# Loading each expert's weights in three transfers, spreading the low parts anew, and starting TensorE on constants earlier, in a fused convolution, attention and expert kernel

## The chip, the cores and the metric

The kernel runs on one core of a Trainium2 chip. The metric is the device time of one execution in microseconds (us); a smaller number is better. The kernel before took 234.52 us as the median of three runs (233.04 to 238.59).

## What is computed

The input x is a batch of 8 images with 192 channels and 16 x 16 pixels, in float32. Three stages follow one another:

```python
x = x + conv1x1(concat(gn(x), corr(gn(x))))   # gn over 32 groups; corr: 28 products of a normalised pixel with neighbours
t = tokens(x)                                 # 8 images x 256 tokens x 192
t = t + softmax(causal(q @ k.T / sqrt(192))) @ v   # q, k, v from the layer-normed t
g = ln(t) @ Wg.T + bg; e = argmax(g)          # one of 8 experts for each token, weight 1
t = t + (silu(ln(t) @ W1[e].T) * (ln(t) @ W2[e].T)) @ W3[e].T   # inner width 469
```

## The kernel before

Each engine has an instruction stream of its own, written out by hand, and the streams meet only at semaphores. SyncE (SP) issues the direct transfers, GpSimd (POOL) the indirect ones.

**Split products.** TensorE reads rounded numbers ("fp32r"). To keep the accuracy of float32, an operand is split into a high part (a rounded copy) and a low part (the original minus the high part), and TensorE sums several products of parts. The eight experts' weights, 1,324 KB each, arrive as float32 in one of two staging places (`stage[:, e % 2]`, 2,648 columns: 940 for channels 0 to 127 of W1 and W2, 940 for the remaining 64 channels in two copies, 768 for W3) and are written split into `wall[:, e]`. ScalarE writes the three high parts (`weights_hi`, lines 549, 551 and 554; semaphores `wall_hi`, `wall_hiq`, `wall_hi3`). GpSimd writes the low parts of the first and the third range (`weights_lo`, lines 434 and 437; `wall_lo` after both), and VectorE turns the second copy in the second range into low parts (`leftover`, line 837; `wall_q`). For experts 6 and 7 all low parts are made by VectorE later, in the expert stage, in six pieces each (`low_weights`, lines 821, 824, 829).

**Staging.** A place is free once the expert that lies in it has been split. SP waits in order for `wall_lo` and `wall_q` of expert e - 2 and then issues the whole of expert e (`weights_in`, line 300, loop of lines 336 to 339). Expert 0 is loaded earlier in four quarters, between the images' own transfers. ScalarE's `weights_hi` waits for the one semaphore of the place (line 547).

**Start.** SP issues the image transfers and the constants. POOL fills constants (lines 372 to 375, the tile `taps` last), and counts each on `filled`. TensorE waits for the fourth, then runs `keep_busy(3)` on `taps` (line 1336): products of constants into a bank that nobody reads, each seen as two instructions of 384 columns. Then come `group_sums(0)` (line 1141, the sums of the group norm of images 0 and 1, which VectorE's `group_factors` at line 728 waits for), `keep_busy(5)`, and `group_sums(1)` for images 2 to 4.

**Convolution stage.** Twelve steps, pipelined over the images: group norm and split (lines 515, 523, 738), neighbour products (1205 to 1209), norms, a round trip of the products through memory to shear them (`gram_to`, `taps_from`), convolution.

**Attention stage.** `step(t)` for t from 1 to 9 works on image t's projections and image t - 1's softmax. ScalarE's order in a step is: copy of the turned image (559), `weights_hi(1)` and `weights_hi(2)` of expert t - 1, the exponentials (585, 586), copies (564, 592), the norm of the next image (613), values (570, 573), `weights_hi(0)` of expert t. TensorE fills in with unread products (`fill`, line 1278). At t = 4, 6, 7, 8 and 9 VectorE also computes gates and positions of tokens, and POOL scatters the token rows by expert.

**Expert stage.** 23 slots of 128 tokens, at least one for each expert. In slot j (`ffn_step`) TensorE turns the previous slot's hidden rows (line 1429), multiplies by W1 and W2 (1146 to 1150, 2 x 5 products of 470 columns), turns the next slot's tokens (1446) and multiplies the previous slot's hidden values by W3 (1468, 1469). VectorE writes the low part HL of the hidden values (1084), the product gh (1089), the low part FL of the tokens (1092), the norm of the slot after next (1078, 1079) and the output rows (1105, 1107). VectorE's pieces of `low_weights` stand at the end of its part of slots 0 to 5, two in each: expert 6 in slots 0 to 2, expert 7 in slots 3 to 5. In slot 0 TensorE has `fill(8)` between the products and the turning.

## Time and profile before

| | |
|---|---|
| median of 3 runs | 234.52 us (233.04 to 238.59) |
| profiled execution, its own time | 233.54 us |
| its span, first to last instruction | 231.7 us |
| TensorE busy | 209.1 us, 90% |
| VectorE busy | 171.4 us, 74% |
| ScalarE busy | 113.9 us, 49% |
| GpSimd busy | 105.3 us, 45% |
| share of the chain that ended last | TensorE 59%, VectorE 16%, POOL 6%, DMA 6%, ScalarE 5% |

The profiled execution lies 1.0 us below the median of the three runs. The 1.84 us between its time and its span lie outside the instructions. A share of busy time is a mean over stages with different limits: the convolution stage ends near 60 us, the attention stage near 126 us, and the expert stage takes the rest. Part of TensorE's busy time is unread products.

### The profile page before, as it was taken

To read this page: it belongs to the slowest core of one execution; us is meant where nothing else is said; L and a number is where in the kernel's file an instruction comes from. 1 tells how busy PE (TensorE), PEld (TensorE's weight loads), DVE (VectorE), ACT (ScalarE), POOL (GpSimd) and SP (SyncE) were. 2 spreads that over 40 slices of the span, in tenths; PEclk is the share of its full clock that TensorE was granted. 3 is DMA by queue.
4 is the path that set the end of the run, shared out by engine and by line. 5 is a ranking of instruction groups with operands and counts; after the bars stand their busy time and mean duration, and the time that the engine had idled before them with its cause. 6 is when DMAs were issued, how large, how long until landed. Compare 5 with 4: busy or idle time off the path is not lost.

```text
span 231.7 us, 4547 instructions
## 1 busy us (share of the span) xinstructions
PE 209.1 (90%) x1331; PEld 182.4 (79%) x1331; DVE 171.4 (74%) x559; ACT 113.9 (49%) x244; POOL 105.3 (45%) x133
## 2 busy tenths in 40 slices
PE   6999799989899969998888799999999999999950
PEld 3686588968799958887665688898999999999940
DVE  3577897768399769699877789997767686868640
ACT  2276585175499697996640134343343333343410
POOL 4245756545439996896665103223131313131221
PEclk9999999999999999999999999999999999999995
DMA  6992247665730663647212332332001000000000
GB/s 218 366 350 87 83 126 187 170 219 165 252 135 0 237 234 117 221 188 259 81 52 63 80 86 70 93 83 78 21 14 37 17 34 20 34 17 22 33 20 0
DMA packets 16343, 26.46 MB, mean 114 GB/s; under 512 B 3795, under 2 KB 12673, under 8 KB 15424
## 3 DMA queue, kind: packets, MB, share of 16 engines
q1 hardware_dynamic: 14448, 22.65, 30.7%
q0 software_dynamic: 1872, 3.52, 4.4%
q8 instruction: 12, 0.20, 0.4%
q14 instruction: 11, 0.09, 0.2%
HBM read 19.76 MB, written 6.76 MB: 114 GB/s over the span
## 4 chain that ended last, share of the span: by engine, by line
PE 59%; DVE 16%; POOL 6%; issue 6%; DMA 6%; ACT 5%; POOLq 1%; DVEq 0%; ACTq 0%
PE bank L1468 8%; PE bank L1146 4%; PE bank L1333 4%; PE bank L1150 4%; PE bank L1149 4%; PE bank L1148 4%; PE bank L1147 4%; PE bank L1429 4%; PE bank L1469 3%; DMA stage<-in_w_all 2%; PE bank L1446 2%; PE bank L1192 2%; DMA taps_sb<-near_rows 2%; DMA out_rows<-yo,rows 1%; PE bank L1141 1%
## 5 line engine op out<-in xcount | busy, mean ns | idle before, releaser
L498 POOL DMA_INDIRECT out_rows<-yo,rows x23 | 23.2, 1011 | 76.9 <-DVE yo L1107 61.5
L1468 PE MATMUL bank<-wall,HH 128*128 (+1 forms) x88 | 28.1, 374 | 0.3 <-issue 0.3
L667 ACT ACTIVATE HH<-bank 128x512 fp32r<-128x512 f32 x23 | 13.8, 599 | 27.8 <-PE bank L1429 27.7
L1089 DVE TENSOR_TENSOR gh<-gh,bank 128x470 f32<-128x470 f32 x23 | 14.8, 645 | 14.5 <-PE bank L1150 14.4
L673 ACT ACTIVATE FH<-bank 128x256 fp32r<-128x256 f32 x23 | 8.9, 385 | 27.5 <-PE bank L1446 27.5
L1469 PE MATMUL bank<-wall,HL 128*128 (+1 forms) x88 | 22.1, 251 | 0.0
L1146 PE MATMUL bank<-wall,FH 128*128 (+1 forms) x46 | 19.3, 419 | 1.6 <-DVE FL L1092 1.6
L464 POOL DMA_INDIRECT token_rows<-rows,posi x16 | 16.9, 1055 | 7.3 <-issue 4.0
L670 ACT ACTIVATE gh<-bank 128x470 f32<-128x470 f32 x23 | 13.0, 565 | 13.1 <-PE bank L1150 13.1
L1278 PE MATMUL bank<-mH 128*128 128x512 f32 x73 | 19.3, 400 | 0.0
L1084 DVE TENSOR_TENSOR HL<-bank,HH 128x512 fp32r<-128x512 f32 x23 | 15.9, 691 | 3.6 <-ACT HH L667 3.4
L1150 PE MATMUL bank<-wall,FL 128*128 (+1 forms) x46 | 17.3, 376 | 0.0
L1149 PE MATMUL bank<-wall,FH 128*128 (+1 forms) x46 | 17.2, 375 | 0.0
L1148 PE MATMUL bank<-wall,FL 128*128 (+1 forms) x46 | 17.2, 375 | 0.0
L1147 PE MATMUL bank<-wall,FH 128*128 (+1 forms) x46 | 17.2, 374 | 0.0
L1468 PEld LDWEIGHTS bank<-wall,HH 128*128 128x128 f32 x88 | 16.5, 188 | 0.8 <-issue 0.8
L1469 PEld LDWEIGHTS bank<-wall,HL 128*128 128x128 f32 x88 | 16.8, 191 | 0.0
L434 POOL TENSOR_TENSOR wall<-stage,wall 128x940 fp32r<-128x940 f32 x6 | 13.6, 2261 | 3.0 <-ACT wall L549 1.8
L1278 PEld LDWEIGHTS bank<-mH 128*128 128x128 f32 x73 | 13.1, 188 | 2.1
L1429 PE MATMUL bank<-small_sb,gh 128*128 128x128 f32 x92 | 13.8, 272 | 0.0
L515 ACT ACTIVATE f32t<-xcm,gnb,grs 128x256 f32<-128x256 f32 x16 | 8.7, 594 | 9.6 <-POOL gnb L392 9.6
L437 POOL TENSOR_TENSOR wall<-stage,wall 128x768 fp32r<-128x768 f32 x6 | 12.8, 2136 | 0.0
(247 smaller groups left out, 647.4 us busy)
## 6 DMA issues: line engine op xcount, KB each, us to landing
stage<-in_w_all SPq DMA_DIRECT2D x7, 1324.0 KB, 5.7
rows<-token_rows SPq DMA_DIRECT2D x23, 98.0 KB, 2.0
near_rows<-gram SPq DMA_DIRECT2D x8, 243.0 KB, 3.2
xcm<-in_x_cm SPq DMA_DIRECT2D x2, 768.0 KB, 8.3
rows<-in_x_tm SPq DMA_DIRECT2D x1, 1536.0 KB, 14.0
stage<-in_w_all SPq DMA_DIRECT2D x4, 331.0 KB, 4.0
token_rows<-emptyt SPq DMA_DIRECT2D x3, 294.0 KB, 4.2
taps_sb<-near_rows SPq DMA_DIRECT2D x8, 103.0 KB, 2.1
```

Source lines behind the costliest of these rows:

```text
L464: pool.indirect_dma_start(out=xs, out_offset=bass.IndirectOffsetOnAxis(ap=posi[:, j:j + 1].bitcast(U32), axis=0), in_=rows[:, j], in_offse ...
L498: pool.indirect_dma_start(out=out, out_offset=bass.IndirectOffsetOnAxis(ap=rows[:, j, C + 2:C + 3].bitcast(U32), axis=0), in_=yo[:, par], ...
L1084: nc.vector.tensor_tensor(HL[:, 1 - par].rearrange("p k x -> p (k x)"), bank[5][:], HH[:, 1 - par].rearrange("p k x -> p (k x)").bitcast(F ...
L1146: nc.tensor.matmul(dst, xh_a, y_a, start=True, stop=False)
L1147: nc.tensor.matmul(dst, xh_a, yl_a, start=False, stop=False)
L1148: nc.tensor.matmul(dst, xl_a, y_a, start=False, stop=False)
L1149: nc.tensor.matmul(dst, xh_b, y_q, start=False, stop=False)
L1150: return nc.tensor.matmul(dst, xl_b, y_q, start=False, stop=not more)
L1278: nc.tensor.matmul(bank[6][:], mH[:, 0:P], mH[:], start=True, stop=True)
L1429: mm = nc.tensor.transpose(bank[5][:, P * k:P * (k + 1)], gh[:, 1 - par, P * k:P * (k + 1)], ident)
L1468: nc.tensor.matmul(dst[:, 0:2 * C], HH[:, 1 - par, k], w(0, P, c0, c0 + 2 * C), start=(k == 0), stop=False)
L1469: mm = nc.tensor.matmul(dst[:, 0:C], HL[:, 1 - par, k], w(0, P, c0, c0 + C), start=False, stop=(k == FT - 1))
```

## The change

Each expert from 1 on is issued in three transfers, the three ranges of the staging place, each with a semaphore of its own; from expert 2 on, each is issued as soon as that range of the expert before has been read. POOL gets a further semaphore, `wall_lo_a`, after its first subtraction. Low pieces 4 and 5 of expert 6 move to the steps of slots -1 and 0 (so slot 0 has three pieces), expert 7's first four pieces move to slots 2 and 3, and its last two stand singly in slots 4 and 5; the waits at the head of `low_weights` are now issued in each call. POOL fills `taps` first, TensorE starts after it, with `keep_busy(6)` in place of 3, and `fill(8)` in slot 0 becomes `fill(5)`. Expert 0 keeps its quarters, under a semaphore of its own.

```diff
+        PARTS = (slice(0, W12), slice(W12, 2 * W12), slice(2 * W12, STAGE))
...
-            def weights_in(e):
-                sp.dma_start(stage[:, e % 2], w_all[e]).then_inc(stage_in[e % 2], 16)
+            def weights_in(e, part):
+                c = PARTS[part]
+                sp.dma_start(stage[:, e % 2, c], w_all[e][:, c]).then_inc(stage_in[e % 2][part], 16)
...
-            weights_in(1)
+            for part in range(3):
+                weights_in(1, part)
 
             for e in range(2, EXPERTS):
+                sp.wait_ge(wall_lo_a, e - 1)
+                weights_in(e, 0)
+                sp.wait_ge(wall_q, e - 1)
+                weights_in(e, 1)
                 sp.wait_ge(wall_lo, e - 1)
-                sp.wait_ge(wall_q, e - 1)
-                weights_in(e)
+                weights_in(e, 2)
...
         def _(pool):
+            nc.gpsimd.memset(taps[:].rearrange("p b h c -> p (b h c)"), 1.0).then_inc(filled, 1)
             nc.gpsimd.memset(half_c[:], -0.5).then_inc(filled, 1)
             nc.gpsimd.memset(emptyt[:], 0.0).then_inc(filled, 1)
             nc.gpsimd.memset(gram[:].rearrange("p b h c -> p (b h c)"), 0.0).then_inc(filled, 1)
-            nc.gpsimd.memset(taps[:].rearrange("p b h c -> p (b h c)"), 1.0).then_inc(filled, 1)
-            pool.wait_ge(filled, 2)
+            pool.wait_ge(filled, 3)
...
-                nc.gpsimd.tensor_tensor(w[:, W12:2 * W12], raw[:, 0:W12], w[:, 0:W12].bitcast(F32), ALU.subtract)
+                nc.gpsimd.tensor_tensor(w[:, W12:2 * W12], raw[:, 0:W12], w[:, 0:W12].bitcast(F32), ALU.subtract).then_inc(wall_lo_a, 1)
...
-                sc.wait_ge(stage_in[e % 2], 16 * (e // 2 + (1 if e % 2 else FIRST_PARTS)))
+                if e == 0:
+                    sc.wait_ge(first_in, 16 * FIRST_PARTS)
+                else:
+                    sc.wait_ge(stage_in[e % 2][part], 16 * ((e + 1) // 2))
...
+                ve.wait_ge(wall_hi, e + 1)
+                ve.wait_ge(wall_hiq, e + 1)
+                ve.wait_ge(wall_hi3, e + 1)
+                ve.wait_ge(wall_lo, e)
                 for n in pieces:
-                    if n == 0:
-                        ve.wait_ge(wall_hi, e + 1)
...
                 if j == -1:
                     ffn_step(j, 1, False, False, True)
                     table_slots()
+                    low_weights(EXPERTS - 2, (4,))
                 elif j == 0:
                     ffn_step(j, 0, False, True, False)
                     norm_slot(1, 1, 1)
+                    low_weights(EXPERTS - 2, (5,))
                     ffn_step(j, 0, False, False, True, 2)
...
-                if 0 <= j < 3:
+                if 0 <= j < 2:
                     low_weights(EXPERTS - 2, (2 * j, 2 * j + 1))
-                elif 3 <= j < 6:
-                    low_weights(EXPERTS - 1, (2 * j - 6, 2 * j - 5))
+                elif 2 <= j < 6:
+                    low_weights(EXPERTS - 1, ((0, 1), (2, 3), (4,), (5,))[j - 2])
...
-            pe.wait_ge(filled, 4)
-            keep_busy(3, taps[:].rearrange("p b h c -> p (b h c)"))
+            pe.wait_ge(filled, 1)
+            keep_busy(6, taps[:].rearrange("p b h c -> p (b h c)"))
...
                 if j == 0:
-                    fill(8)
+                    fill(5)
```

## Rows read from the trace of the kernel before

**Rows 1.** The page: busy time, share of the span and instructions of each engine.
```profile
PE 209.1 (90%) x1331; PEld 182.4 (79%) x1331; DVE 171.4 (74%) x559; ACT 113.9 (49%) x244; POOL 105.3 (45%) x133
```
**Rows 2.** The waits: engine, line, who was waited for, total us, times, longest us.
```profile
ACT wall L549 <- DMA stage<-in_w_all: 2.2, 2, 1.8
```
**Rows 3.** Timeline of ScalarE, end of attention step 3: start us, duration us.
```profile
81.21 0.99 ACT L549 ACTIVATE wall<-stage 128x940 fp32r<-128x940 f32 x1 [1.80 <-DMA stage<-in_w_all]
```
**Rows 4.** Timelines of POOL and VectorE: expert 1's low parts.
```profile
70.47 2.21 POOL L434 TENSOR_TENSOR wall<-stage,wall 128x940 fp32r<-128x940 f32 x1
72.63 2.76 POOL L437 TENSOR_TENSOR wall<-stage,wall 128x768 fp32r<-128x768 f32 x1
...
71.29 2.38 DVE L837 TENSOR_TENSOR wall<-stage,wall 64x940 fp32r<-64x940 f32 x1
```
**Rows 5.** The chain that ended last, at expert 3's transfer: start us, us.
```profile
75.42 5.71 DMA stage<-in_w_all
```
**Rows 6.** The issues of transfers: count, KB each, median us from issue to landing.
```profile
stage<-in_w_all SPq DMA_DIRECT2D x7, 1324.0 KB, 5.7
...
stage<-in_w_all SPq DMA_DIRECT2D x4, 331.0 KB, 4.0
```
**Rows 7.** Timeline of TensorE in attention step 4.
```profile
83.70 0.39 PE L1234 MATMUL bank<-XH,mH 128*128 128x256 f32 x1 [1.52 <-DVE XH L800]
```
**Rows 8.** The chain that ended last, turning of gh in slots 2 to 4.
```profile
142.22 0.44 PE bank L1429 x4
...
146.56 0.44 PE bank L1429 x4
...
150.52 0.44 PE bank L1429 x4
```
**Rows 9.** Timeline of all engines in slot 2, around the last two pieces of expert 6.
```profile
143.16 1.21 DVE L829 TENSOR_TENSOR wall<-stage,wall 64x470 fp32r<-64x470 f32 x2
...
144.40 0.69 DVE L1084 TENSOR_TENSOR HL<-bank,HH 128x512 fp32r<-128x512 f32 x1
...
145.16 0.19 PEld L1468 LDWEIGHTS bank<-wall,HH 128*128 128x128 f32 x1 [0.36 <-issue]
```
**Rows 10.** Timeline of all engines in slot 0.
```profile
131.38 2.02 PE L1278 MATMUL bank<-mH 128*128 128x512 f32 x8
131.58 0.65 DVE L1089 TENSOR_TENSOR gh<-gh,bank 128x470 f32<-128x470 f32 x1 [0.83 <-PE bank L1150]
...
132.43 0.31 DVE L1079 TENSOR_SCALAR xf<-rows 128x64 f32<-128x64 f32 x1
...
133.23 0.38 PE L1446 MATMUL bank<-small_sb,xf 128*128 128x128 f32 x2
...
134.07 0.42 DVE L1092 TENSOR_TENSOR FL<-bank,FH 128x256 fp32r<-128x256 f32 x1 [1.33 <-ACT FH L673]
```
**Rows 11.** Timeline of the first 15 us: constants' products, group sums, and what waits.
```profile
1.79 0.45 POOL L375 MEMSET taps_sb<- 128x416 f32 x1
...
2.29 4.21 PE L1333 MATMUL bank<-taps_sb 128*128 128x384 f32 x6 [2.29 <-POOL taps_sb L375]
...
6.29 1.72 PE L1141 MATMUL bank<-mq,small_sb 128*128 128x8 f32 x8
...
11.06 1.16 PEld L1333 LDWEIGHTS bank<-small_sb 128*128 128x128 f32 x4 [0.17 <-issue]
...
12.68 0.96 PE L1141 MATMUL bank<-mq,small_sb 128*128 128x12 f32 x8
...
13.67 0.25 DVE L728 TENSOR_REDUCE mv<-bank 128x6 f32<-128x12 f32 x2 [0.74 <-PE bank L1141]
14.24 0.68 DVE L738 TENSOR_TENSOR f<-f32t,f 128x512 fp32r<-128x512 f32 x1
```
**Rows 12.** Granted clock by stretch: us, busy by engine, clock, DMA share, GB/s.
```profile
2.30:3.30 1.00, 1.00 (x2) 0.70 (x3) 0.00 (x0) 0.00 (x0) 0.69 (x5) 1.00 0.90 340
...
120.00:220.00 100.00, 96.85 (x575) 86.90 (x576) 77.55 (x213) 35.05 (x68) 26.09 (x28) 1.00 0.16 47
```

More of the change, by code:

```diff
@@ L242, in build @@
         cm_in = [sem(f"cm_in{g}") for g in range(len(GANGS))]
-        stage_in = [sem("stage_in0"), sem("stage_in1")]
+        first_in = sem("first_in")
+        stage_in = [[sem(f"stage_in{par}{part}") for part in range(3)] for par in range(2)]
+        wall_lo_a = sem("wall_lo_a")
+        PARTS = (slice(0, W12), slice(W12, 2 * W12), slice(2 * W12, STAGE))
         empty_out = sem("empty_out")
@@ L329, in _ @@
                     c = slice(n * (b - 2), n * (b - 1))
-                    sp.dma_start(stage[:, 0, c], w_all[0][:, c]).then_inc(stage_in[0], 16)
+                    sp.dma_start(stage[:, 0, c], w_all[0][:, c]).then_inc(first_in, 16)
                 if 4 <= b < 4 + HEAD_PARTS:
@@ L760, in take_gram @@
                 ve.wait_ge(rn_ready, b + 1)
-                ve.wait_ge(filled, 3)
+                ve.wait_ge(filled, 4)
                 if b >= 2:
@@ L812, in low_weights @@
                 raw3 = raw[:, 2 * W12:STAGE].rearrange("p (k c) -> p k c", c=C)
+                ve.wait_ge(wall_hi, e + 1)
+                ve.wait_ge(wall_hiq, e + 1)
+                ve.wait_ge(wall_hi3, e + 1)
+                ve.wait_ge(wall_lo, e)
                 for n in pieces:
-                    if n == 0:
-                        ve.wait_ge(wall_hi, e + 1)
-                        ve.wait_ge(wall_hiq, e + 1)
-                        ve.wait_ge(wall_hi3, e + 1)
-                        ve.wait_ge(wall_lo, e)
                     if n < 2:
@@ L1333, in keep_busy @@
                     nc.tensor.matmul(bank[6][:, 0:3 * P], some[:, 0:P], some[:, 0:3 * P], start=True, stop=True)
-            pe.wait_ge(filled, 4)
-            keep_busy(3, taps[:].rearrange("p b h c -> p (b h c)"))
+            pe.wait_ge(filled, 1)
+            keep_busy(6, taps[:].rearrange("p b h c -> p (b h c)"))
             pe.wait_ge(group_in, 16)
```

## The prediction

> **What bounds the kernel now.** I read the shares of the engines first. TensorE is busy for 90% of the span [rows 1], but many of its products are unread, so the share alone does not say that it is the bound. I therefore went to the waits and the timelines of the three places that the change touches. For the attention stage the list of waits shows ScalarE stopped at line 549 by a transfer of weights, 2.2 us in two waits, the longer one 1.8 us [rows 2]. The timeline places it: ScalarE stands still for 1.80 us until expert 3 has landed, and only then reads it [rows 3]. Behind that instruction in ScalarE's queue stands the copy of the turned image of step 4, for which VectorE and then TensorE wait: TensorE idles for 1.52 us at its projection [rows 7]. The expert stage is bound by TensorE, with a slot of about 3.9 us; the turning of gh comes 4.34 us after the one before in slot 3 and 3.96 us in slot 4 [rows 8], and the reason lies in slot 2. In the first 15 us the chain runs through the group sums and through constants' products that stand ahead of them in TensorE's queue [rows 11].
>
> **Three transfers per expert.** Expert 3's place is free when expert 1 has been split. GpSimd's first subtraction ends at 70.47 + 2.21 = 72.68, VectorE's leftover at 71.29 + 2.38 = 73.67, GpSimd's second at 72.63 + 2.76 = 75.39 [rows 4]. The whole expert is issued then, at 75.42, and takes 5.71 us [rows 5], to 81.13. The first third would be issued near 72.7, the second near 73.7, and only the last at 75.4. No row shows a third alone. A quarter (331 KB) took 4.0 us and the whole 5.7 us [rows 6]. A third has 481 KB (128 x 940 x 4 bytes), the last 393 KB, so the bounds are 4.0 and 5.7 us, the first from transfers that ran beside others. I take 4.3, near the quarter. ScalarE wants the first range at 81.21 - 1.80 = 79.41 [rows 3]. It lands at 77.0, or at 78.4 by the upper bound: no wait by either. The second range is read 1.6 us later, after the 0.99 us of that row and a copy, and lands at 78.0 to 79.4. The last lands at 79.7 to 81.1, and is wanted near 81.9. The wait goes under both bounds.
>
> The rule that speaks against this is in the Trainium skill, "DMA: Bandwidth & Descriptors", section "Bandwidth": collect transfers to at least 1 MiB, since each pays a fixed cost (about 2.0 us there, plus bytes at 436 GB/s). By it a third would take an estimated 3.1 us and the first would land at 75.8, and if SP had to pay the three fixed costs one behind the other the last would land some 2 us later; SP does not wait for landings between the thirds, so the sum would stay as it is.
>
> What is late next? VectorE (its line 799, behind the copy) and TensorE follow ScalarE's copy. TensorE cannot come forward by more than its idle time of 1.52 us plus a start-up of about 0.15 us after a wait, since products stand before it [rows 7]; ScalarE comes forward by 1.80. I take 1.7. GpSimd does not come forward in step 4: it works from 70 us on without a pause. What it makes for the gates is wanted later, and the next low parts are wanted only for transfers that have slack now, because of the thirds. The second wait at line 549, 2.2 - 1.8 = 0.4 us for expert 7, goes too, but ScalarE then waits for VectorE in step 8, so it counts as nothing; without that cover it would be 0.4. The added transfers and waits on SP stand ahead of nothing but each other until the first slots are loaded some 15 us later. The other steps of attention keep their lengths. **Term: -1.7 us** (bounds -1.3, where half of a gate step takes some of it, and -1.9).
>
> **Low parts spread anew.** In slot 2 VectorE's two pieces run from 143.16 for 1.21 us; the low part HL starts right behind them at 144.40, takes 0.69 us, and TensorE's weight load for W3 has idled for 0.36 us until then [rows 9]. The same pattern stands once more in slot 5 (two in all). A single piece of about 0.6 us ends before HL can start, so slots 4 and 5 lose nothing. The pairs (0, 1) and (2, 3) stand in slots 0 to 3. A pair (0, 1) was in slot 3 before, and its slot took 3.96 against 4.34 us [rows 8]. Gain: 2 x (4.34 - 3.96) = 0.76 us. The two moved pieces need cover. In slot -1 VectorE idles for 0.83 us before gh [rows 10]; a piece is 1.21 / 2 = 0.6 us. In slot 0 it idles for 1.33 us before FL [rows 10], again more than a piece. Both are covered; if a piece were stretched beside GpSimd's work as the leftover was (2.38 us for one operation of twice the columns, so 1.2 for one piece [rows 4]), each would stick out by up to 0.4 us, but GpSimd is idle there after its last scatter. The four waits now issued per call are for things long done. **Term: -0.8 us** (bounds 0 and -0.8).
>
> **Fill of 5 for 8 in slot 0.** Eight unread products take 2.02 us from 131.38, and the turning comes at 133.23 [rows 10]. Three fewer would free 0.6 us, but the turning reads xf, which is whole at 132.43 + 0.31 = 132.74 [rows 10]. So it moves from 133.23 to about 132.8, and FH, FL and the products follow, since VectorE's piece ends by 133.4, before FL is due at 133.6. **Term: -0.4 us** (bounds 0 and -0.45).
>
> **The start.** Filling `taps` took 0.45 us [rows 11] and moves to the head, so TensorE starts near 1.2 instead of 2.29. It has twelve instructions ahead of the group sums instead of six. These are spaced 0.64 us at first (six in 4.21 us, the last one's end included) and half as much from about 10.9 us on, where four weight loads take 1.16 us [rows 11]; this is the lower and the upper of the two levels, 1.2 and 2.4 GHz, by durations, though the granted clock reads 1.00 in both [rows 12]. Before, all six instructions ran at the lower level, then the eight sums, and the rise came among the ten that followed. In the changed kernel, with k of the twelve at the lower level, the sums start at 1.2 + 0.64 k + 0.32 (12 - k). No row shows k. I bound it by 5 and 11 and take 8, so the sums start at 6.6 to 8.6, likeliest 7.6, instead of 6.29. At the upper level they take about 0.8 instead of 1.72 us (the eight of the second group took 0.96, end included [rows 11]), so they end at 7.4 to 9.4, where it was 8.01 before. The ten products after them take 3.2 us, where before the span from 8.0 to 12.68 was 4.7. `group_sums(1)` is through at 11.4 to 13.4 instead of 13.64, so VectorE's wait of 0.74 us goes [rows 11]; the split of image 1 at 14.24, where VectorE's unbroken work begins, moves by -0.85 us (it has the group factors and image 0's split before it, all moved by at most that) to +0.9 us. Near the middle: **term -0.1 us**. "TensorE: Matmul & The Clock Gate" of the Trainium skill, Part 1, says that the moment of the rise differs from run to run of one kernel; no run here shows this yet, and it only supports leaving both ends in the range.
>
> **Sum.** -1.7 - 0.8 - 0.4 - 0.1 = -3.0. From the profiled execution's 233.54 us that is 230.5. This execution lies 1.0 below the median of the three runs shown, and the changed kernel's median may lie above its best in the same way, so I name 230.8 us, 1.6% below 234.52. About 2% (4.7 us, so below 229.8 or above 239.2) is what a measurement of this kernel can tell from no change.
>
> **Rivals.**
>
> *The start becomes later (15%).* If the clock rises no sooner than before, at 10.9, the twelve products end at 1.2 + 12 x 0.64 = 8.9, the sums still take 1.5, and the chain of image 0 is 2.4 later; the split of image 1 moves by +2.0. For it: six products did not raise the clock. Against: it rose among ten that followed one another, and the new run has twelve. Time: 233.5 - 2.9 + 2.0 = 232.6.
>
> *Attention gives the gain back (12%).* The wait goes, but a gate step of VectorE or GpSimd's unbroken work sets steps 5 to 9, and the stage ends where it did. For: GpSimd cannot start expert 3's low parts earlier. Against: after 81 us every wait on the path was for VectorE, which itself waited for ScalarE's late copy. Time: 233.5 - 1.3 = 232.2.
>
> *The start gains more (15%).* Only five of the twelve run at the lower level; or other runs of the kernel before have a late rise that the new one never has. Time: 233.5 - 2.9 - 0.85 = 229.8, or 229.3 with both ends of the attention and slot terms.
>
> *Slower (4%).* Fewer unread products in slot 0 leave TensorE two pauses near 0.5 us close together, and its clock falls to the lower level in the expert stage. A slot at half the clock costs up to another 3.9 us, so one slot makes the kernel slower than before, and three make it over 2% slower: 230.5 + 3 x 3.9 = 242. Against: a pause of 1.52 us [rows 7] was followed by instructions of the usual length, and the clock reads 1.00 over the whole stretch from 120 to 220 [rows 12].
>
> *My forecast (54%)*, with its own range 229.9 to 231.8.
>
> **Range and chances.** 229.2 to 233.3 takes in the first three rivals but leaves out the slower one and the far ends of the others. Faster by over 2%: the greater gain, and a part of the forecast's lower end, 0.22. Slower by over 2%: 0.03. Within 2%: 0.75.
>
> **What would show it.** Right: no wait of ScalarE for a transfer of weights after 60 us; the three thirds of expert 3 issued near 72.7, 73.7 and 75.4; no idle time of some 0.36 us before line 1468 in slots 2 and 5; `xf` as the last thing before the turning in slot 0; TensorE's spacing halved before 8 us. Wrong: a third that takes over 6.7 us to land; a leftover of VectorE stretched to over 2 us at a new place, since steps shifted by 1.7 us meet GpSimd's work in another order; or a later `group_factors` that shifts the whole convolution stage.

## The result, and the profile after

The changed kernel takes 234.33 us (median of 20 runs, 232.76 to 235.99), the kernel before 233.98 us beside it (20 runs, 231.85 to 238.59). The ratio is 1.0048 with a 95% interval of 1.0027 to 1.0068: about 1.1 us slower, where 230.8 us and a range of 229.2 to 233.3 us were forecast. Ratios, here and below, leave disturbed executions out and medians don't; where the two differ the ratio counts.

The page after, its first part, the code loads of its part 3 and the weights of its part 6 (count, KB each, median us to landing). They answer to [rows 1] and [rows 6].
```profile
PE 208.1 (90%) x1334; PEld 181.5 (78%) x1334; DVE 174.0 (75%) x559; ACT 113.7 (49%) x244; POOL 104.8 (45%) x133
...
q8 instruction: 12, 0.20, 0.4%
...
stage<-in_w_all SPq DMA_DIRECT2D x14, 470.0 KB, 4.0
stage<-in_w_all SPq DMA_DIRECT2D x7, 384.0 KB, 4.1
```
A third lands in 4.0 us, so the transfers did what was forecast. VectorE is busy 2.6 us longer with the same 559 instructions: that is the first sign of where the gain went.

To find where the two executions part, I compared the start of one instruction per step: ScalarE's first exponential of each attention step (line 585 before, 596 after), the turning of gh (the first and the last group of four products that the chain shows, at 138.30 and 217.59 us before), and the end of the span.

| stretch | before | after | difference |
|---|---|---|---|
| to the exponential of step 1 | 62.26 | 62.56 | +0.30 |
| step 1 to step 4 | 22.10 | 20.20 | -1.90 |
| step 4 to step 5 | 7.95 | 10.77 | +2.82 |
| step 5 to step 8 | 20.97 | 20.72 | -0.25 |
| step 8 to the first turning | 25.02 | 24.69 | -0.33 |
| first to last turning | 79.29 | 78.57 | -0.72 |
| last turning to the end | 14.11 | 14.49 | +0.38 |
| span | 231.7 | 232.0 | +0.3 |

Every term that was forecast as a gain is there, and a single step takes the largest one back.

Timeline of ScalarE after, from the end of step 3 to step 5 (start us, duration us; in brackets the idle time before it and its releaser). It answers to [rows 3].
```profile
79.59 0.99 ACT L560 ACTIVATE wall<-stage 128x940 fp32r<-128x940 f32 x1
...
82.76 0.40 ACT L596 ACTIVATE rows<-rows,nmx 128x128 f32<-128x128 f32 x1
...
93.53 0.40 ACT L596 ACTIVATE rows<-rows,nmx 128x128 f32<-128x128 f32 x1 [4.11 <-DVE nmx L919]
```
The 1.80 us wait for expert 3's weights is gone. In its place ScalarE waits 4.11 us for VectorE one step later. The same row of before:
```profile
92.31 0.40 ACT L585 ACTIVATE rows<-rows,nmx 128x128 f32<-128x128 f32 x1 [1.28 <-DVE nmx L909]
```
Timelines of GpSimd (POOL) and then VectorE after, between the two exponentials:
```profile
84.68 1.83 POOL L445 TENSOR_TENSOR wall<-stage,wall 128x768 fp32r<-128x768 f32 x1
...
87.52 2.19 POOL L442 TENSOR_TENSOR wall<-stage,wall 128x940 fp32r<-128x940 f32 x1
89.68 2.70 POOL L445 TENSOR_TENSOR wall<-stage,wall 128x768 fp32r<-128x768 f32 x1
...
84.93 2.04 DVE L860 SCALAR_TENSOR_TENSOR bank<-rows,small_sb 128x8 f32<-128x8 f32 x4
...
88.14 2.56 DVE L847 TENSOR_TENSOR wall<-stage,wall 64x940 fp32r<-64x940 f32 x1
```
and the same of before:
```profile
84.42 1.83 POOL L437 TENSOR_TENSOR wall<-stage,wall 128x768 fp32r<-128x768 f32 x1
...
89.01 2.55 POOL L434 TENSOR_TENSOR wall<-stage,wall 128x940 fp32r<-128x940 f32 x1 [1.77 <-ACT wall L549]
...
86.54 0.64 DVE L850 SCALAR_TENSOR_TENSOR bank<-rows,small_sb 128x8 f32<-128x8 f32 x4
...
88.35 1.14 DVE L837 TENSOR_TENSOR wall<-stage,wall 64x940 fp32r<-64x940 f32 x1
```
Read them against each other. Before, the gate's four operations start at 86.54, after GpSimd's subtraction has ended (84.42 + 1.83 = 86.25), and the leftover of expert 3 starts at 88.35, ahead of GpSimd's next subtraction at 89.01; both take their usual time, and the subtraction is the one that is stretched, to 2.55. After, the gate comes 1.6 us earlier and meets the subtraction of 84.68: it ends only behind it (86.51). The leftover then starts 0.6 us behind the subtraction of 87.52 and stands until 89.71. Cost: (2.04 - 0.64) + (2.56 - 1.14) = 2.82 us, exactly the lengthening of step 5. [Rows 4] show the same in the kernel before, at another place: a leftover of 2.38 us beside the subtraction of 70.47. The rule for this is in the Trainium skill, "SBUF — State Buffer", section "Who interferes with whom": a VectorE instruction with two inputs in SBUF and a GpSimd instruction that reads SBUF cannot run together, and the one that issues second waits for the first to finish. The trace agrees, in both directions: in each of these pairs the later one carries the stretch. It isn't so for every pair of the kind: in the convolution stage of the kernel before, a VectorE subtraction of this sort takes its usual 0.69 us at 23.53 while GpSimd is in a 6-column operation (`grs`, 23.23 to 24.66).

Slot 0 and the turnings after, from the timeline and the chain that ended last. They answer to [rows 10] and [rows 8].
```profile
131.75 0.65 DVE L839 TENSOR_TENSOR wall<-stage,wall 64x470 fp32r<-64x470 f32 x1
...
132.37 1.36 PE L1290 MATMUL bank<-mH 128*128 128x512 f32 x5
...
133.42 0.31 DVE L1089 TENSOR_SCALAR xf<-rows 128x64 f32<-128x64 f32 x1
...
133.78 0.44 PE L1458 MATMUL bank<-small_sb,xf 128*128 128x128 f32 x2
```
```profile
138.94 0.44 PE bank L1441 x4
142.88 0.44 PE bank L1441 x4
146.98 0.44 PE bank L1441 x4
150.90 0.44 PE bank L1441 x4
```
`xf` is now what the turning waits for, as forecast. Slot 3 takes 4.10 us instead of 4.34, and the idle time of [rows 9] before the W3 weight load is gone.

The start after: GpSimd, TensorE, VectorE. It answers to [rows 11].
```profile
0.70 0.45 POOL L380 MEMSET taps_sb<- 128x416 f32 x1 [0.29 <-POOLq L1560]
...
1.84 6.32 PE L1345 MATMUL bank<-taps_sb 128*128 128x384 f32 x12 [1.84 <-POOL emptyt L382]
8.00 0.95 PE L1153 MATMUL bank<-mq,small_sb 128*128 128x8 f32 x8
8.81 3.47 PE L1345 MATMUL bank<-small_sb 128*128 128x384 f32 x10
12.13 1.06 PE L1153 MATMUL bank<-mq,small_sb 128*128 128x12 f32 x8
...
14.80 0.69 DVE L749 TENSOR_TENSOR f<-f32t,f 128x512 fp32r<-128x512 f32 x1 [0.26 <-ACT f L531]
```
`taps` is full at 1.15, but TensorE begins at 1.84, not at 1.2. The sums begin at 8.00, and the split of image 1 at 14.80 instead of 14.24.

The last stretch after, from the chain that ended last; the same transfer of before follows it.
```profile
222.77 3.80 DMA out_rows<-yo,rows
```
```profile
222.86 3.44 DMA out_rows<-yo,rows
```
It is the last-but-one transfer of results, which the last one has to wait for. What decides its length turned out to be another transfer (below).

### The profile page after: what moved, and what is told of

The parts are those of the page before. It is cut to its first block, busy times and chain, and to the rows that moved or that the text cites. A ratio compares the mean times of both kernels' runs of the same rounds, so it can differ in the third digit from the quotient of the medians.

```text
span 232.0 us, 4573 instructions
## 1 busy us (share of the span) xinstructions
PE 208.1 (90%) x1334; PEld 181.5 (78%) x1334; DVE 174.0 (75%) x559; ACT 113.7 (49%) x244; POOL 104.8 (45%) x133
## 4 chain that ended last, share of the span: by engine, by line
PE 53%; DVE 21%; ACT 9%; issue 7%; POOL 6%; DMA 2%; POOLq 1%; DVEq 0%; ACTq 0%
PE bank L1480 7%; PE bank L1158 4%; PE bank L1162 4%; PE bank L1160 4%; PE bank L1161 4%; PE bank L1159 4%; PE bank L1441 4%; PE bank L1481 3%; PE bank L1345 3%; PE bank L1458 2%; POOL spread L419 2%; DMA out_rows<-yo,rows 2%; DVE wall L847 2%; PE bank L1204 2%; DVE bank L860 1%
## 5 line engine op out<-in xcount | busy, mean ns | idle before, releaser
L506 POOL DMA_INDIRECT out_rows<-yo,rows x23 | 22.6, 983 | 76.9 <-DVE yo L1117 59.8
L472 POOL DMA_INDIRECT token_rows<-rows,posi x16 | 16.3, 1022 | 7.4 <-issue 4.1
L681 ACT ACTIVATE gh<-bank 128x470 f32<-128x470 f32 x23 | 13.0, 565 | 13.1 <-PE bank L1162 13.1
L1290 PE MATMUL bank<-mH 128*128 128x512 f32 x70 | 18.6, 401 | 0.0
L1290 PEld LDWEIGHTS bank<-mH 128*128 128x128 f32 x70 | 12.5, 188 | 2.1
L445 POOL TENSOR_TENSOR wall<-stage,wall 128x768 fp32r<-128x768 f32 x6 | 13.7, 2284 | 0.0
```

The source lines that it names most:

```text
L472: pool.indirect_dma_start(out=xs, out_offset=bass.IndirectOffsetOnAxis(ap=posi[:, j:j + 1].bitcast(U32), axis=0), in_=rows[:, j], in_offse ...
L506: pool.indirect_dma_start(out=out, out_offset=bass.IndirectOffsetOnAxis(ap=rows[:, j, C + 2:C + 3].bitcast(U32), axis=0), in_=yo[:, par], ...
L1290: nc.tensor.matmul(bank[6][:], mH[:, 0:P], mH[:], start=True, stop=True)
```

## The experiments

The theory after this reading, **order**: the freed ScalarE moves VectorE's gate and leftover into GpSimd's subtractions. Its first rival, **traffic**: 25 transfers instead of 11 are themselves the loss. All ratios are to the kernel before, run beside them.

### One part of the change at a time

e1: thirds alone, the diff's parts for `weights_in`, `wall_lo_a` and the waits. e2: `low_weights` and `fill(5)` alone. e3: the start alone (`taps` filled first, six products instead of three).

> Only the three transfers per expert, on the kernel before. My theory (order): the 1.9 us that ScalarE no longer waits are lost again in step 5, because VectorE's gate inputs (two operands in SBUF) and its leftover of expert 3 now start while GpSimd is subtracting, and stand still until GpSimd's instruction ends (2.04 for 0.64 us and 2.56 for 1.14 us in the changed kernel). Then this kernel is 0.5 to 1.3 us slower than the kernel before, with both stretched instructions in its trace. Rival (traffic): the thirds' transfers themselves disturb VectorE's reads; it gives the same time here but the stretch would follow the landing of transfers. Second rival (start): the loss comes from the convolution stage; then this kernel is 1.5 to 1.9 us faster.

> Only the low pieces spread anew and the fill of 5 for 8. My theory: the gain seen in the changed kernel (0.36 in slot 0, 0.68 in slots 2 and 5) stands by itself: 1.0 to 1.2 us faster than the kernel before. Rival: it is there only in that one profile, and the fill or the pieces cost what they give: within 0.3 us of the kernel before.

> Only the start: constants filled first, six products for three. From the changed kernel's profile: group sums end 0.9 us later, the rest of the convolution stage 0.3 us later, so 0.3 us slower (0 to 0.6). Rival: the moment at which the clock rises differs so much between runs that the early products pay on the median: 0.3 to 1.0 us faster.

| | median | ratio | interval |
|---|---|---|---|
| e1 thirds | 234.66 | 1.0046 | 1.0010 to 1.0081 |
| e2 pieces and fill | 230.69 | 0.9882 | 0.9854 to 0.9910 |
| e3 start | 234.83 | 1.0073 | 1.0040 to 1.0105 |

Thirds alone lose 1.1 us. VectorE's rows of e1:
```profile
85.16 2.04 DVE L861 SCALAR_TENSOR_TENSOR bank<-rows,small_sb 128x8 f32<-128x8 f32 x4
...
88.36 2.56 DVE L848 TENSOR_TENSOR wall<-stage,wall 64x940 fp32r<-64x940 f32 x1
```
The collision comes with the thirds and needs neither of the other two parts, and the loss is in the range expected for it (0.5 to 1.3 us). The start loses 1.7 us, where 0.3 was expected from the one profile. Pieces and fill bring 2.8 us (0.0118 x 233), where 1.2 was forecast: too much, and this was followed up below.

### Out of GpSimd's way

e4: the changed kernel, and the one row of `bg` that the first gate step reads from `small_sb` is copied once into an unused corner of bank 7. The first gate, the one of step 4, then has one input in SBUF instead of two.
```
+bg_bank = bank[7][:, 400:400 + EXPERTS]
+nc.vector.tensor_copy(bg_bank, c2("bg")[:, 0:EXPERTS]).then_inc(bg_kept, 1)
-in1=c2("bg")[:, 0:EXPERTS]
+in1=bg_bank if g == 0 else c2("bg")[:, 0:EXPERTS]
```


> The whole change, and the gate bias of the first gate is read from a PSUM bank instead of SBUF, so that the four gate instructions of step 4 have one operand in SBUF. Theory (order): they take 0.64 us instead of 2.04, the leftover of expert 3 then starts at about 86.9, before GpSimd's next subtraction at 87.5, and takes 1.14 instead of 2.56. The attention stage keeps the 1.9 us: 2.6 to 2.9 us faster than the whole change, 2.0 to 2.6 us faster than the kernel before (231.5 to 232). Rival (traffic): the gate instructions stay near 2 us or the leftover stays near 2.5 us, and the time stays within 0.5 us of the whole change.

Measured: 231.10 us, ratio 0.9915 (0.9890 to 0.9941). VectorE in e4:
```profile
85.30 0.62 DVE L863 SCALAR_TENSOR_TENSOR bank<-rows,bank 128x8 f32<-128x8 f32 x4
...
87.09 1.13 DVE L848 TENSOR_TENSOR wall<-stage,wall 64x940 fp32r<-64x940 f32 x1
```
GpSimd's subtraction runs beside it from 84.98 to 86.83, as in the changed kernel, and the gate no longer stands. The leftover follows 1.4 us sooner and is ahead of the next subtraction, so it isn't stretched either; here GpSimd comes second, and its small operation at 87.11 takes 1.70 us instead of 0.72. From the exponential of step 1 to that of step 5 it takes 91.05 - 62.88 = 28.17 us, where before took 30.05 and the changed kernel 30.97: so the 1.9 us are kept. By the ratios e4 is 3.1 us under the changed kernel, where 2.6 to 2.9 were expected.

e7: the bank alone, on the kernel before.

> The kernel before with the gate's row kept in bank 7 and nothing else. Order theory: in before the gate's operation takes 0.64 us already, so nothing is to be had: the time of before within 0.3 us (0.999 to 1.001). If keeping the row in the bank is good by itself (one operand less from SBUF, wherever the step falls): 0.3 us or more faster.

Measured: 233.20 us, ratio 0.9990 (0.9954 to 1.0026). The bank is worth nothing without the thirds.

e14: thirds and bank together, nothing else.

> Thirds alone and the gate's row kept in bank 7. Order theory: the gate in 0.62 us whatever GpSimd does, attention 1.9 us shorter, 231.9 us, ratio 0.992. Traffic theory: ratio 1.005 as thirds alone, since the bank by itself gave nothing (0.999).

Measured: 231.19 us, ratio 0.9897 (0.9853 to 0.9942). With the very transfers of e1 the kernel is 2.4 us faster than before instead of 1.1 slower. This speaks plainly against traffic. The two ratios lie 3.5 us apart, of which the rows of the collision account for 2.8.

### Two controls that hold ScalarE back

e5: thirds, but expert 3's three transfers are issued together behind both semaphores.

> As thirds alone, but the three transfers of expert 3 are issued together where the one transfer stands in the kernel before (behind both semaphores of the low parts); all the others stay in thirds. Order theory (the loss comes because the freed ScalarE puts the gate of the first slots and a low piece of VectorE beside a GpSimd subtraction): with expert 3 late, ScalarE waits about 1.8 us for it again in step 4, the gate's operation takes 0.6 us and the low piece of expert 3 1.1 us as before, and the time is that of before within 0.5 us. Traffic theory (the many smaller transfers themselves slow the kernel): the loss of thirds alone, 1.1 us (ratio 1.005), stays, since there are as many transfers as there.

Measured: 234.60 us, ratio 1.0064 (1.0028 to 1.0100). It didn't make the condition that it was meant to make: ScalarE waited 0.74 us, not 1.8. Of the three transfers, issued from 74.10 us on, the first two land after 3.5 and 4.7 us, before they are wanted, and only the last, after 6.9 us, is late (one of 1,324 KB took 5.7). VectorE met GpSimd at yet another phase:
```profile
83.93 1.42 DVE L867 SCALAR_TENSOR_TENSOR bank<-rows,small_sb 128x8 f32<-128x8 f32 x4
...
86.52 3.16 DVE L854 TENSOR_TENSOR wall<-stage,wall 64x940 fp32r<-64x940 f32 x1
```
The leftover started 0.05 us behind a subtraction of 2.21 us (86.47) and took 2.0 us on top of its 1.14. As a test of traffic this run decides nothing; it shows that the price goes with the phase.

e13: thirds, and ScalarE makes its first copy of expert 3's weights three times, so that it is busy where it used to wait.
```
+for i in range(2 if e == 3 else 0):
+    if i: sc.wait_ge(twice, i)
+    nc.scalar.activation(w[:, 0:W12], raw[:, 0:W12], ACT.Copy).then_inc(twice, 1)
+if e == 3: sc.wait_ge(twice, 2)
```


> Thirds alone, and ScalarE makes its first copy of expert 3's weights three times, so the 1.8 us that it waited for DMA in the kernel before it is now busy; all transfers are as in thirds alone. Order theory: step 4 starts at 84.4 us as before, the gate takes 0.64 us and the low piece of expert 3 1.1 us again, and the time is that of before within 0.4 us (ratio 0.998 to 1.002). Traffic theory: the transfers still cost, ratio 1.005 as thirds alone, or more with the added copies.

Measured: 234.26 us, ratio 1.0041 (1.0005 to 1.0077). In the trace the two operations take what the order theory says:
```profile
85.74 0.64 DVE L867 SCALAR_TENSOR_TENSOR bank<-rows,small_sb 128x8 f32<-128x8 f32 x4
...
87.55 1.14 DVE L854 TENSOR_TENSOR wall<-stage,wall 64x940 fp32r<-64x940 f32 x1
```
and steps 1 to 5 take 91.50 - 61.32 = 30.18 us (before 30.05). The time does not: it should have been that of before, the ratio lies 0.1 to 1.8 us above it, and in time e13 can't be told from e1. The profiled execution (233.26 us) is no slower than that of before (233.54), with its last-but-one result transfer at 3.95 us, 0.5 longer. So the collision is shown in the rows, and its removal in e4 and e14, but this control doesn't confirm its price: some loss of up to 1.8 us goes with the thirds here and not in e14, which gained 2.4 us where 1.9 were expected. The granted clock gives a hint. The six executions of e13 with a mean granted clock of 0.985 or more have a median of 233.56 us, and the fifteen such executions of the kernel before beside them 233.54; the other six of e13 have 235.19. So the loss of e13 lies in the executions of the lower clock. This grouping was made afterwards, and it isn't traced what lowered the clock there; the cause stays open.

### The start

e8: the change's start with three products instead of six.
```
-keep_busy(6, taps...)
+keep_busy(3, taps...)
```


> The change's start with three products of taps_sb instead of six: the constants are still set first and TensorE still begins at 1.84 us. Queue theory (the three added products stand ahead of the first group sums, which are ready at 6.1 us but begin at 7.3 to 8.4): with three, TensorE is free at about 5.7 us, the sums begin at 6.1 to 6.3 us as before, and the time is that of before within 0.5 us. Rival (the earlier work of TensorE and GpSimd, not the number of products, costs it): the loss of the start alone, 1.7 us (ratio 1.007), stays.

Measured: 232.56 us, ratio 0.9995 (0.9968 to 1.0022). TensorE in e8:
```profile
1.84 3.81 PE L1333 MATMUL bank<-taps_sb 128*128 128x384 f32 x6 [1.84 <-POOL emptyt L374]
6.13 1.03 PE L1141 MATMUL bank<-mq,small_sb 128*128 128x8 f32 x8 [0.48 <-DVE mq L718]
```
The three added products were the loss: e3 and e8 differ in nothing else, by 1.8 us, and the transfer at the end is long in both (3.72 and 3.63 us). With three, TensorE is free 0.48 us before the sums' input is ready; with six the sums stand behind them in TensorE's queue.

The added products did buy the faster clock for the sums every time, but too dearly. In all five profiled executions with six products of `taps` (the changed kernel, e3, e4, e15, e17) the eight sums of the first group take 0.95 to 0.96 us. In the fourteen with three (the kernel before and thirteen others) they take 1.03 us six times and 1.36 to 1.85 eight times, as in [rows 11] and in e11, which has the start of e8:
```profile
6.11 1.85 PE L1153 MATMUL bank<-mq,small_sb 128*128 128x8 f32 x8
```
With six, though, the sums begin at 7.3 to 8.5 us instead of 6.0 to 6.3. They end at 8.2 to 9.5, against 7.1 to 8.1. The split of image 1 follows: 14.80, 14.10, 15.18, 14.17 and 15.31 us with six, mean 14.7, against 12.9 to 14.7 with three, mean 13.7. So the profiles show 1.0 us of the 1.7 to 1.8; where the rest arises was not traced. The one profiled execution of before that the forecast started from (14.24) was at the late end.

### The surplus of e2: a load of code

e2's last-but-one result transfer took 2.12 us, against 3.44 before. In the windows after 220 us the list of DMA queues of the kernel before has one 16 KB packet on queue 8, kind `instruction`, which lands in the same microsecond (224 to 225); that of e2 has none. The **code** theory: the last load of TensorE's program falls into this transfer and holds it up. The DMA queues of the kernel before, from 224.2 to 225.15 us and then from 225.15 to 225.5, show how:
```profile
q8 instruction: 1, 0.02, 6.1%
q0 software_dynamic: 45, 0.00, 2.8%
```
```profile
q0 software_dynamic: 3, 0.00, 1.1%
```
The transfer consists of 48 small packets. The packet of code starts at 224.28 us and takes 0.93, to 225.21; 45 of the 48 start beside it, and the last three only as it ends. The landing comes 1.1 us after the end of the code. In e2 all 48 start within 0.2 us and the landing comes 0.4 us after the last. All twelve profiles with a load there look so: three packets wait for its end, and the landing comes 1.1 us after it.

e9: the kernel before with `fill(5)` for `fill(8)`. e10: the pieces of e2 with `fill(8)`.

> The kernel before with five filling products instead of eight ahead of slot 0, and nothing else. Code theory (the 12th load of 16 KB of code on queue 8 lands at 224.8 us, while the last but one indirect transfer of results is on its way, and stretches it from 2.1 to 3.4 us; three products fewer in TensorE's program do without that load): 11 such loads, the transfer in 2.1 us, and 1.3 us for that beside 0.4 us for the fill, so 232.0 us, ratio 0.993. Fill theory (only TensorE's time ahead of slot 0 counts): 0.4 us, ratio 0.998, and the transfer stays over 3.4 us.

> The pieces spread as in the change, but with eight filling products as before. Code theory: 12 code loads and the long transfer again, so only the pieces' own 0.7 to 0.8 us of the 2.8 us that pieces and fill brought together: 232.9 us, ratio 0.997. If the pieces themselves brought the 2.8 us: 231.3 us or less, ratio 0.990.

Measured: e9 231.63 us, ratio 0.9905 (0.9872 to 0.9937), 11 loads and the transfer in 2.12 us. Three unread products are worth 2.2 us, where their own time explains 0.4. e10: 231.81 us, ratio 0.9919 (0.9883 to 0.9956). Here the expectation failed: TensorE's program has 1331 recorded products as before, yet the transfer took 2.12 us, and the twelfth load came at 232 us, behind the span's end. The size fits (0.7 for the pieces and 1.3 for the transfer make 2.0; 1.9 measured), but the load behind the end doesn't seem to be free: e10's profiled execution has 2.8 us between its time and its span, instead of the usual 1.8, and so have nine of its twelve executions (2.55 to 2.89), against eight of 168 of the other changed kernels (over 2.3). With 0.8 us for that the sum is 1.2, still within the interval (1.0 to 2.7). Why the load moved, and not in all executions, is open.

e15: the changed kernel with `fill(2)` for `fill(5)`.

> The changed kernel with two filling products ahead of slot 0 instead of five, so TensorE's program is three products shorter, as in the runs whose transfer took 2.1 us. Code theory: no load of code between 220 and 226 us, the last-but-one indirect transfer in 2.1 us instead of 3.8, so 1.7 us less than the changed kernel, ratio to before 0.997. Fill theory: the slot's input of 0.17 us wait is all that is left to gain, so nothing, ratio 1.004.

Measured: 234.19 us, ratio 1.0018 (0.9984 to 1.0052), load at 225 us, transfer 3.42 us. I had counted wrongly: a float32 product of the start is recorded as two (six products, x12), so this kernel has the 1331 recorded products of the kernel before, not 1328. Two more runs cross that count from either side.

e16: e12 (below) with three more products behind TensorE's last one, where nothing waits for them. e17: the changed kernel with six fewer (`fill(2)` for `fill(5)`, `fill(9)` for `fill(12)`).

> The changed kernel with three products at the start and the bank (228.5 us, 1328 products recorded, transfer 2.06 us), and three more products of mH appended behind TensorE's last one, where nothing waits for them: 1331 products. Code theory: the load of 16 KB of code near 221 us is back and the last-but-one transfer of results takes 3.4 to 3.9 us, so 1.3 to 1.8 us more, 230.0 us, ratio 0.985. Otherwise: 228.5 us, ratio 0.979, transfer 2.1 us.

> The changed kernel with six filling products fewer (two instead of five ahead of slot 0, nine instead of twelve after attention): 1328 products recorded. Code theory: no load of code between 220 and 226 us, the transfer in 2.1 us, 1.5 us less than the changed kernel, ratio 0.997. Otherwise: the transfer in 3.4 to 3.8 us and ratio 1.002 to 1.005.

Measured: e16 230.48 us, ratio 0.9847 (0.9796 to 0.9897), 1.4 us over e12 by the ratios. e17 232.63 us, ratio 0.9966 (0.9931 to 1.0001), 1.9 us under the changed kernel by the ratios. For each, page part 1 and the transfer, e16 first:
```profile
PE 206.8 (91%) x1331; PEld 180.5 (79%) x1331; DVE 171.7 (75%) x560; ACT 113.8 (50%) x244; POOL 104.6 (46%) x133
...
218.70 3.84 DMA out_rows<-yo,rows
```
```profile
PE 207.2 (90%) x1328; PEld 180.6 (78%) x1328; DVE 174.0 (75%) x559; ACT 113.7 (49%) x244; POOL 104.7 (45%) x133
...
223.22 2.06 DMA out_rows<-yo,rows
```
And the DMA queues of e16 and then of e17 in the window that holds this transfer:
```profile
q8 instruction: 1, 0.02, 0.9%
q0 software_dynamic: 96, 0.00, 0.7%
```
```profile
q0 software_dynamic: 130, 0.13, 4.6%
```
Both expectations are met; by time alone e16's is not shown, since the intervals of e12 and e16 overlap, but e17's interval lies clear of that of the changed kernel. Over all profiles, the six kernels with 1328 recorded products (e2, e6, e9, e11, e12, e17) have no load there and 2.06 to 2.12 us; those with 1331 to 1337 have one and 3.42 to 3.95 us, but for e10.

### The parts put together

e11: the changed kernel with three products at the start. e6: thirds, pieces and fill, and bank, with the old start. e12: the changed kernel with three products at the start, and the bank.

> The changed kernel with three products of taps_sb instead of six at the start. Queue theory and code theory together: the first group sums begin at 6.1 to 6.3 us again and TensorE's program is three products shorter, so the transfer takes 2.1 us: 1.2 to 1.7 us and 1.7 us less than the changed kernel, 231.2 us, ratio to before 0.991. If the start costs nothing here and only the attention's collision does: 234.3 us, ratio 1.005.

> Thirds, the low parts and fill of the change, the gate's row kept in bank 7, and the start as before. Order theory: attention 1.9 us shorter (exponential of step 1 to step 5 in 28.2 us), expert stage as in pieces alone, start as before, so 229.5 us, ratio 0.984, and about 1.5 us under the changed kernel with the gate's row in its bank. If the parts don't add up (the shorter attention puts other operations beside GpSimd's): as pieces alone, 230.7 us.

> The changed kernel with three products at the start and the gate's row kept in bank 7. All theories added: 229.1 us as thirds, pieces and bank with the old start, since the earlier start gave nothing by itself, within 0.4 us; ratio 0.984 and about 2 us under the changed kernel with six products and the bank (231.1 us). If the early start is worth something once nothing else is in its way: 228.7 us or less.

| | median | ratio | interval |
|---|---|---|---|
| e11 | 232.41 | 0.9890 | 0.9827 to 0.9953 |
| e6 | 229.11 | 0.9844 | 0.9811 to 0.9876 |
| e12 | 228.45 | 0.9788 | 0.9738 to 0.9838 |

e11 met its 231.2 us within its interval (0.9890 x 233.83 = 231.3). e6 met its forecast of 0.984 as well. e12 came out below its 229.1 us, at the value named for an early start that pays once nothing else is in its way; its interval overlaps that of e6, so this last step (0.7 us by the medians) is likely and not shown. e12 is the fastest kernel here, 2.1% under the one before, and holds every idea of the change with two repairs.

## Why the prediction was wrong

**Three transfers: right to the landing, wrong behind it.** No wait of ScalarE for weights is left, and the thirds of expert 3 are issued at 73.01, 74.00 and 75.72, as forecast but for the 0.3 us by which the whole stage is later. A third lands in 4.0 us (4.3 taken; the estimate of 3.1 that stood beside it was too short), and steps 1 to 4 got 1.90 us shorter (1.7 taken). The step that failed is "the other steps of attention keep their lengths": step 5 grew by 2.82 us. The prediction had both halves in hand. It read the stretched leftover of [rows 4], and it named, as a sign of being wrong, a leftover stretched to over 2 us at a new place. But it looked for stretch only where pieces were moved by the edit, and not where they were moved by the gain. The moved gate at 84.9 could have been laid beside GpSimd's subtraction, which the prediction itself said would not come forward. The rival "attention gives the gain back" (12%) had the place, with a price of all of the gain; the price was the gain and 0.9 us more. (One sum of the prediction is off: for the rival "the start gains more", both ends of the other terms give 233.54 - 1.9 - 0.8 - 0.45 - 0.85 = 229.5, not 229.3.)

**Low parts: right.** First to last turning -0.72 us, forecast -0.76, and the idle times before the W3 loads are gone in slots 2 and 5. That it is so near has some luck in it: the two places gave 0.24 (4.34 to 4.10) and 0.42 us (4.34 to 3.92) instead of 0.38 each. **Fill: right**, -0.33 us against -0.4.

**The start: wrong in size and in sign.** Forecast -0.1, bounds -0.85 and +0.9; alone it cost 1.7 us (0.9 to 2.4 by its interval), and e8 puts that on the three added products. In the profiled execution alone the split of image 1 moved by +0.56, inside the bounds. The value of k was no fault: seven of the twelve instructions ran at the lower level there, and five to nine in the five executions, where 8 was taken. Three other things were at fault. TensorE begins at 1.84, not at 1.2, so the sums begin at 8.00. The forecast looked to the second group's sums, whose wait does go; but with six products the split of image 1 comes 1.95 us after that of image 0 in all five, so the first group sets it, and that one is later. And the comparison was made with one execution whose clock rose late. With three products the second group's sums begin at 10.3 to 13.1 us in the profiled executions, with six at 11.4 to 12.7; against the early ones six products can only delay. The rival "the start becomes later" (15%) had the sign, but by another route: it had the clock rise only at 10.9 us, and in the changed kernel the spacing halves before 7 us.

**What no step had.** The tail: fill 5 for 8 shortens TensorE's program by three recorded products and by itself removes the late load of code, worth 1.3 us by the transfers' lengths in e2 and e9 and 1.4 to 1.9 by the ratios of e16 and e17 (the latter with six unread products less). The start adds six and brings it back. So the changed kernel lost a gain that pieces and fill had alone, by three products added at the other end of the program. The three parts' ratios multiply to 1.0000; with the load of code back (1.4 of 233 us) that is 1.006, and 1.0048 was measured.

## What to carry to other kernels

When a change takes a wait away, shift every later operation of the freed engines by the gain and lay it beside the other engines' long operations: on VectorE and GpSimd, two inputs in SBUF against a read of SBUF cost whoever comes second about the rest of the first. Taking one input from a bank instead repairs that instruction at any phase seen here (0.62 us beside the subtraction in e4 and e14); the leftover, which kept its two inputs, escaped only by its place. Before adding unread products, see what stands behind them in the queue, in an execution whose clock rises early as well as in the profiled one. And when two versions differ by more than their parts, look in the list of DMA queues for `instruction` packets beside the last transfers.

## What the runs showed of the hardware

- A 16 KB load of code in the tail stretches a transfer of 48 small packets from 2.1 us to between 3.4 and 3.9 us: the last three packets start only when it ends. Three matmuls more or fewer in the program decide whether it is there. What makes the load fall there rather than later (e10) is open.
- After an idle time of TensorE its clock can fall. In e2's profiled execution TensorE idled 1.74 us in step 4 while the weights of expert 3 were late, and 2 us later its products were spaced 0.21 us instead of 0.11; the granted clock of that stretch reads 0.50, the lower level (the last fence, columns as in [rows 12]):
```profile
82.76 0.39 PE L1235 MATMUL bank<-XH,mH 128*128 128x256 f32 x1 [1.74 <-DVE XH L800]
...
85.54 0.41 PE L1250 MATMUL bank<-vwH,XL 128*128 128x208 f32 x1
85.75 0.41 PE L1251 MATMUL bank<-vwH,XH 128*128 128x208 f32 x1
```
```profile
85.00:90.50 5.50, 5.50 (x34) 5.26 (x33) 3.34 (x13) 3.18 (x8) 2.44 (x4) 0.50 0.18 33
```
Its step 5 took 10.11 us, against 7.95 in the profiled execution of before, which has nearly the same idle time (1.52 us, [rows 7]) without the fall. If the fall came of that idle time, the wait that the thirds remove costs 1.8 us in one execution and an estimated 4 in another (1.8 and the 2.2 of step 5). The collision that took its place may do the same one step later: in e11 the exponentials of steps 5 and 6 are 7.82 us apart, against 6.73, with a granted clock of 0.69 from 93.6 to 98 us; in the changed kernel's own profile the clock stays at 1.00 there. This may be why medians and profiled executions disagree by up to a microsecond; it was not tested by itself.
- At the program's start TensorE began 0.7 us after its constants were full (1.15 and 1.84 us); what it waited for isn't in the profile.
